# Routed experts of a two-layer model: counts loaded before the last puts, and two buffers for gathered rows

## What is computed

```python
# layer 0: 8 experts, width 1024, 4 of them for each token
router_logits = jnp.einsum('bsd,de->bse', x, router_w)
routing_weights = jax.nn.softmax(router_logits, axis=-1)
topk_weights, topk_indices = jax.lax.top_k(routing_weights, 4)
topk_weights = topk_weights / jnp.sum(topk_weights, axis=-1, keepdims=True)
h = jax.nn.gelu(jnp.einsum('bsd,edh->bseh', x, up_w))   # tanh form
expert_outputs = jnp.einsum('bseh,ehd->bsed', h, down_w)
gathered = jnp.take_along_axis(expert_outputs, topk_indices[:, :, :, None], axis=2)
output = jnp.sum(topk_weights[:, :, :, None] * gathered, axis=2)

# layer 1: 8 experts, width 1024, 2 of them for each token
gate_logits = x @ gate_w + gate_b
topk_vals, topk_idx = jax.lax.top_k(gate_logits, 2)
topk_w = jax.nn.softmax(topk_vals, axis=-1)
comb = jnp.sum(onehot * topk_w[..., None], axis=2)
h = jax.nn.gelu(jnp.einsum('btd,edf->ebtf', x, w1) + b1[:, None, None, :], approximate=False)
y = jnp.einsum('ebtf,efd->ebtd', h, w2) + b2[:, None, None, :]
output = jnp.einsum('ebtd,bte->btd', y, comb)

# the whole, for each layer
x = x + jnp.tanh(g_ffn[layer]) * ffn(_layernorm(x, axis=-1), ...)
```

## Time and profile before

| | us |
|---|---|
| median of 3 runs | 1602.8 |
| lowest and highest | 1600.75, 1604.12 |
| the profiled execution, its own time | 1604.2 |
| its span in the trace | 1602.3 |

### The profile page before, as it was taken

The page is one execution under the profiler, slowest core; times in us unless marked ns, Lnnn a source line. Parts: engine busy times, 40 slices in busy tenths (PEclk is TensorE's granted clock), DMA queues, the critical chain, the costliest instruction groups (busy, mean ns, idle before and its releaser), DMA issues. The chain is left out here.

```text
span 1602.3 us, 25436 instructions
## 1 busy us (share of the span) xinstructions
PE 1392.9 (87%) x9908; PEld 1288.8 (80%) x9908; DVE 834.8 (52%) x1654; ACT 713.1 (45%) x1375; POOL 552.5 (34%) x389
## 2 busy tenths in 40 slices
PE   5899989899867999999989995999889678987996
PEld 5776858768647899899889995988888668987996
DVE  3655656655664446446435223556666865455421
ACT  3354444444343454444444443454343425443553
POOL 1200001001025466566565441122120266566543
PEclk8899999999987999999999997998989769998998
DMA  3302031110115343443442223021202165444222
GB/s 128 120 24 67 27 95 43 52 61 27 66 51 156 94 86 81 116 106 92 105 104 47 47 42 100 24 88 41 72 30 80 54 193 119 102 106 109 48 42 35
DMA packets 72147, 123.30 MB, mean 77 GB/s; under 512 B 7440, under 2 KB 53152, under 8 KB 71968
## 3 DMA queue, kind: packets, MB, share of 16 engines
q1 hardware_dynamic: 46816, 81.92, 15.6%
q0 software_dynamic: 25152, 39.01, 13.4%
HBM read 96.12 MB, written 24.79 MB: 75 GB/s over the span
## 5 line engine op out<-in xcount | busy, mean ns | idle before, releaser
L2324 DVE TENSOR_TENSOR m_hidden_lo<-m_act_out,m_hidden_hi 128x512 fp32r<-128x512 f32 x224 | 162.6, 727 | 393.9 <-ACT m_hidden_hi L2267 368.5
L395 PE MATMUL banks<-m_down_hi,m_hidden_hi 128*128 128x256 f32 x896 | 267.9, 299 | 17.5 <-DVE m_hidden_lo L2324 11.3
L395 PE MATMUL banks<-m_down_hi,m_hidden_lo 128*128 128x256 f32 x896 | 263.7, 294 | 1.5 <-issue 1.5
L395 PE MATMUL banks<-m_down_lo,m_hidden_hi 128*128 128x256 f32 x896 | 263.9, 295 | 0.3 <-issue 0.3
L395 PEld LDWEIGHTS banks<-m_down_hi,m_hidden_hi 128*128 128x128 f32 x896 | 181.6, 203 | 22.2 <-issue 20.4
L395 PE MATMUL banks<-m_xt_hi,m_up_hi 128*128 128x256 f32 x640 | 186.6, 291 | 6.4 <-issue 6.4
L395 PE MATMUL banks<-m_xt_lo,m_up_hi 128*128 128x256 f32 x640 | 183.2, 286 | 0.0
L395 PE MATMUL banks<-m_xt_hi,m_up_lo 128*128 128x256 f32 x640 | 183.1, 286 | 0.0
L395 PEld LDWEIGHTS banks<-m_down_hi,m_hidden_lo 128*128 128x128 f32 x896 | 181.1, 202 | 1.7 <-issue 1.7
L395 PEld LDWEIGHTS banks<-m_down_lo,m_hidden_hi 128*128 128x128 f32 x896 | 181.5, 203 | 0.6 <-issue 0.6
L2401 POOL DMA_INDIRECT m_other_block<-rows,list_i x116 | 120.8, 1042 | 148.5 <-DVE list_i L1453 100.6
(11 more groups left out here) (367 smaller groups left out, 3555.0 us busy)
## 6 DMA issues: line engine op xcount, KB each, us to landing
stage<-in_down SPq DMA_DIRECT2D x22, 512.0 KB
stage<-in_ctx_cols SPq DMA_DIRECT2D x26, 402.0 KB
stage<-in_ctx_rows SPq DMA_DIRECT2D x20, 512.0 KB
stage<-in_up SPq DMA_DIRECT2D x20, 512.0 KB
m_stage<-in_up SPq DMA_DIRECT2D x11, 512.0 KB
m_stage<-in_down SPq DMA_DIRECT2D x10, 512.0 KB
rows<-xn SPq DMA_DIRECT2D x8, 528.0 KB, 3.7
stage<-in_ctx_picked SPq DMA_DIRECT2D x8, 512.0 KB
```

The costliest lines, as they stand in the source:

```text
L395: mm = q.e.matmul(dst, a, b, start=first and n == 0, stop=last and n == 2, skip_group_check=True)
L2324: q.e.tensor_tensor(lo, m.act[(n * HP + h) % ACTS], f32(hi), ALU.subtract).then_inc(*hidden_lo.mark((layer, n, h)))
```

## The change

It has two parts.

*Counts.* PE sums the counts of the last batch right after the places. VectorE casts them before mark 0 (vector_count), and each engine loads the eight registers earlier than before: PE between the count's matmul and put 0 (before: behind the 48 downs of block (0, 0)), ScalarE ahead of turning block (0, 1), VectorE when the lists are done, ahead of the next expert's casts, GpSimd before it waits for the lists. The first downs wait for put 3's sum instead of the counts' cast.

*Rows.* The blocks from 2 on take turns in two buffers: m.other for even j, and for odd j the memory of the two onehot tables, which only the route uses. Each has a semaphore and a register that counts what was begun. Block j's rows are gathered in block j - 3, so those of blocks 2 and 3 both in the opening of the expert, which is now written out in gpsimd_opening in a new order. There is one more block gathered for nearly every expert, since it is begun one block further ahead.

The diff, cut to its changed lines and a line beside them:

```diff
         stage_in = [signal(f"stage_in{i}") for i in range(6)]
-        first_in, second_in, other_in = signal("first_in"), signal("second_in"), signal("other_in")
+        first_in, second_in, other_in = signal("first_in"), signal("second_in"), [signal(f"other_in{i}") for i in range(2)]
         adding, added, other_there = signal("adding"), signal("added"), signal("other_there")
...
         lists = sb("lists", [P, E * M])
-        shared = [sb(f"onehot{i}", [P, E * P], F16) for i in range(2)]
-        onehot = [s[:, :].rearrange("p (e q) -> p e q", e=E) for s in shared]
-        pairwise = shared[0][:, :].bitcast(F32)
+        tables = sb("onehot", [P, 2 * E * P], F16)
+        shared = [tables[:, i * E * P:(i + 1) * E * P] for i in range(2)]
+        rows_there = tables[:, 0:2 * BT * ROW].bitcast(F32).rearrange("p (t d) -> p t d", t=BT)
+        onehot = [s.rearrange("p (e q) -> p e q", e=E) for s in shared]
+        pairwise = shared[0].bitcast(F32)
         above, same = (pairwise[:, i * TT * E * E:(i + 1) * TT * E * E].rearrange("p (t a b) -> p t a b", t=TT, a=E)
...
             def scales():
-                m.other = sb(n + "other_block", [P, BT, ROW], F32, st)[:, :, :]
+                m.other = [sb(n + "other_block", [P, BT, ROW], F32, st)[:, :, :], rows_there]
                 m.w_first, m.w_last = ([sb(n + f"{w}{i}", [P, BT], F32, st)[:, :] for i in range(2)] for w in ("w_first", "w_last"))
...
-        def vector_finish_lists(q, layer):
+        def vector_count(q, layer):
             use = ("count", layer)
             q.wait_ge(*route_pe.of(*use))
+            q.wait_ge(*added.of(layer - 1, "all"))
+            q.e.tensor_copy(counts_i[:, :], gen.of(use)[0:1, 0:E]).then_inc(*route_dve.mark(use))
+        def vector_finish_lists(q, layer):
             q.wait_ge(*route_dve.last())
-            q.e.tensor_copy(counts_i[:, :], gen.of(use)[0:1, 0:E]).then_inc(*route_dve.mark(use))
             spare = col("spare").unsqueeze(1).to_broadcast([P, E * NB - 1, BT])
...
             m = exp[layer]
-            return m.other if j > 1 or (e, j) == (0, 0) else m.second if j else m.first
+            return m.other[j % 2] if j > 1 or (e, j) == (0, 0) else m.second if j else m.first
...
                 return numbered(0, 0)
-            return numbered(e, j - 1) if j > 2 else numbered(e - 1, NB - 1) if j == 2 else numbered(e - 1, j)
+            return numbered(e, j - 2) if j > 3 else numbered(e - 1, NB - 4 + j) if j > 1 else numbered(e - 1, j)
...
-                q.wait_ge(*route_dve.of("count", layer))
+                q.wait_ge(*route_dve.of("put", layer, BATCH - 1, TT - 1))
             if layer and f == 0:
...
             tensor_place(q, layer, b)
+            tensor_count(q, layer)
+            held = counts(q, layer)
             for i in range(TT):
                 tensor_put(q, layer, b, i)
-            tensor_count(q, layer)
             for f in range(HT):
...
                 tensor_down(q, layer, 0, 0, f)
-            held = counts(q, layer)
             for e in range(E):
...
             scalar_choose(q, layer, b)
+            held = counts(q, layer)
             scalar_turn_block(q, layer, 0, 1)
-            held = counts(q, layer)
             for e in range(E):
...
             vector_place(q, layer, b)
+            vector_count(q, layer)
             vector_mark(q, layer, b, 0)
...
             vector_finish_lists(q, layer)
+            held = counts(q, layer)
             q.wait_ge(*rows_out[layer].of(layer, b))
...
             convert(q, "d", [quarter(layer, 1, x) for x in range(KD, 4)])
-            held = counts(q, layer)
             for e in range(E):
...
-        others_begun, adds_begun = [0], [0]
+        others_begun, adds_begun = [0, 0], [0]
         def gpsimd_gather(q, layer, e, j):
-            g, there = block_rows(layer, e, j), other_in if j > 1 else second_in if j else first_in
+            g, there = block_rows(layer, e, j), other_in[j % 2] if j > 1 else second_in if j else first_in
             q.wait_ge(*turned_block.of(layer, in_place(e, j)))
             q.wait_ge(*handed.of("w", layer, in_place(e, j)))
-            if j == 2 and (layer or e):
-                q.e.wait_ge(other_in.sem, q.e.snap(others_begun[0]))
+            if j in (2, 3) and (layer or e):
+                q.e.wait_ge(there.sem, q.e.snap(others_begun[j % 2]))
                 q.e.nop().then_inc(*rested.mark())
...
             if j > 1:
-                q.e.reg_add(others_begun[0], others_begun[0], 16 * BT)
+                q.e.reg_add(others_begun[j % 2], others_begun[j % 2], 16 * BT)
...
-            q.e.wait_ge(other_in.sem, q.e.snap(others_begun[0]))
+            q.e.wait_ge(other_in[j % 2].sem, q.e.snap(others_begun[j % 2]))
             q.e.nop().then_inc(*other_there.mark((layer, e, j)))
...
         def gpsimd_block(q, layer, e, j):
-            n, more = numbered(e, j), j == 0 and e + 1 < E
-            gpsimd_added(q, layer, n - 2)
-            if 0 < j < NB - 1:
+            n = numbered(e, j)
+            if j != 1:
+                gpsimd_added(q, layer, n - 2)
+            if j == 0:
+                gpsimd_opening(q, layer, e)
+                return
+            if 1 < j < NB - 1:
                 gpsimd_there(q, layer, e, j + 1)
-            if (e, j) == (1, 0):
+            gpsimd_add(q, layer, e, j)
+            if j + 3 < NB:
+                gpsimd_gather(q, layer, e, j + 3)
+        def gpsimd_opening(q, layer, e):
+            n, following = numbered(e, 0), [quarter(layer, e + 1, x) for x in range(4)] if e + 1 < E else []
+            gpsimd_gather(q, layer, e, 2)
+            gpsimd_gather(q, layer, e, 3)
+            if e == 1:
                 gpsimd_gather(q, layer, 2, 0)
-            if more:
-                convert(q, "p", [quarter(layer, e + 1, x) for x in range(KD)])
+            convert(q, "p", following[0:KD])
             if n:
-                gpsimd_add(q, layer, e, j)
-            if j + 2 < NB:
-                gpsimd_gather(q, layer, e, j + 2)
-            if more:
-                convert(q, "p", [quarter(layer, e + 1, x) for x in range(KD, 4)])
+                gpsimd_add(q, layer, e, 0)
+            gpsimd_there(q, layer, e, 2)
+            convert(q, "p", following[KD:4])
+            if following:
                 gpsimd_gather(q, layer, e + 1, 1)
-                if e and e + 2 < E:
-                    gpsimd_gather(q, layer, e + 2, 0)
-            if j == 0:
-                convert(q, "p", ahead(layer, e - 1))
+            gpsimd_added(q, layer, n - 1)
+            if e and e + 2 < E:
+                gpsimd_gather(q, layer, e + 2, 0)
+            convert(q, "p", ahead(layer, e - 1))
...
             own = [other_there, added]
+            held = counts(q, layer)
             q.wait_ge(*route_dve.of("listed", layer))
...
             gpsimd_gather(q, layer, 1, 0)
-            held = counts(q, layer)
             for e in range(E):
...
             gpsimd_added(q, layer, E * NB - 2)
-            q.e.wait_ge(other_in.sem, q.e.snap(others_begun[0]))
-            q.e.nop().then_inc(*rested.mark())
+            for there, begun in zip(other_in, others_begun):
+                q.e.wait_ge(there.sem, q.e.snap(begun))
+                q.e.nop().then_inc(*rested.mark())
             gpsimd_add(q, layer, E, 0)
...
         def _(e):
-            others_begun[:] = [e.alloc_register("others_begun")]
+            others_begun[:] = [e.alloc_register(f"others_begun{i}") for i in range(2)]
             adds_begun[:] = [e.alloc_register("adds_begun")]
```

## The result

| | before | after |
|---|---|---|
| median, us | 1604.08 (20 runs) | 1609.59 (20 runs) |
| lowest and highest | 1596.47, 1616.07 | 1603.27, 1618.05 |
| the profiled execution, and its span | 1604.2, 1602.3 | 1606.95, 1604.8 |

The changed kernel is slower: the ratio is 1.0037, with a 95% interval of 1.002 to 1.0054. A second comparison, in another session, gave 1.002 (1.0004 to 1.0035). So the loss is 3 to 6 us by the two ratios (0.6 to 8.7 by their intervals).

The account below looks back on a forecast made before the run. The prediction took PE, busy for 87% of the span, to bound the kernel. Its terms, -4.7 (four waits), +0.2 (layer 0's route), +3.1 (layer 1) and 0 (GpSimd's queue), gave 1602.8 - 1.4 = 1601.4 us, range 1596 to 1608.5.

Parts of the forecast that it names:

- The loads, layer 0: Layer 0's route: PE's count loads ahead of put 0 make it 4.1 us later; the route sums to +0.2 us.
- the loads' price is given back at the ups: Layer 0's route: ups only 1.2 us later, then 1.7 us regained at full clock, so -0.5 us.
- The four places: PE's waits on rows before block 3's transposes, experts 2 to 5 of layer 0: earlier gathers save 4.7 of 8.1 us.
- Rival D: The four places don't get shorter, since y and the landing of adds bound them: 1606.1 us, chance 0.09.
- Layer 1: Layer 1's route and first experts: a later PE restart and late rows together cost +3.1 us, between 0 and +5.
- the transposes of (2,0): Layer 1: GpSimd's longer queue gathers block (2,0)'s rows late, so PE waits at its transposes, +1.1 us.
- the held y: Layer 1, expert 0: ScalarE's first y waits for GpSimd, delaying PE's restart before expert 1 by +2.0 us.
- GpSimd's queue: One more pair of gathers in most experts, 2.6 us, nearly fits idle time: 0, up to +3 us.
- rival C: GpSimd's conversions collide with VectorE's hidden_lo in the openings, costing 6.6 us: slower, at 1608 us, chance 0.18.
- The sum: All terms together: -4.7 + 0.2 + 3.1 + 0 = -1.4 us for the whole kernel.

Follow-up runs that it names:

- there_first: The changed kernel with GpSimd's word that the next rows are there put ahead of its wait for the add's landing: 1605.04 us, ratio 1.0007 to the kernel before.
- after_again: The changed kernel measured once more, unaltered, against the kernel before: 1609.08 for 1604.86 us, ratio 1.002.
- rows_only: The changed kernel with its counts' half taken back, keeping two buffers, gathers three blocks ahead and the new opening: 1601.94 us, ratio 0.9988 to the kernel before.
- counts_only: The kernel before with only the counts' half of the change: 1609.59 against 1604.86 us, ratio 1.0031.
- y_early: rows_only with GpSimd's word for each layer's first y given at the start of expert 0's opening: 1600.77 us, ratio 0.998 to the kernel before.
- pe_late: The changed kernel with PE's eight loads behind the 48 downs again: 1599.01 us against 1601.78 for the kernel before, ratio 0.9971.

## Why the prediction was wrong, by its steps

**The loads, layer 0.** Put 0 was forecast 4.1 us later and came 4.2 later (8.9 behind the count's place for 4.7), the downs 3.9 later and came 4.0 later. The step that failed is the next: "the loads' price is given back at the ups: -0.5". The ups came 2.5 us later, not 1.2, because ScalarE split the turned block 2.0 us after its transposes, for 0.6 before (2.0, 1.6 and 3.0 in after, there_first and after_again, which have both halves and PE's loads early, 0.6 in all others; I have no cause that I could show). And the clock gave nothing back. The forecast took the ups at full clock; their first 4.6 us were granted 0.63 and 0.50 after, as they were before (0.63 and 0.50). PE's own time over the route, without idle time, is 37.3 and 38.9 us after, 37.5 and 39.0 before. The route cost +3.1 us, for +0.2 forecast.

**The four places.** Forecast -4.7, measured -0.9, -0.1, -0.8 and 0.0 at the waits (0.46, 2.30, 0.56 and 3.02 are left), -2.7 for the whole stretch, of which 1.4 is idle time. Two steps failed. First, I took the rows to free PE as soon as they were there, and did not ask where GpSimd says so. Its word stands behind the wait for the add, so PE stood until y started. That is shown by there_first. Second, the gain of 1.2 each rested on hidden_lo being ready 2.7 us behind y. That distance was right (710.84 to 713.60 in there_first), but the downs waited for it 2.65 and 3.81 us, because the add is as late as ever. Rival D named this, with 0.09, and the sentence "the change leaves both where they are" had it: where two things are late for one reason, removing one gives nothing. I had read SyncE's issues in the earlier trace rows, and not what released them 0.03 us before.

**Layer 1.** Forecast +3.1, measured +5.0. Of the mechanism the parts were: put 0 as in layer 0 (+3.9), the transposes of (2,0) 0.7 us late for their rows (+1.1 forecast, seen in PE's timeline as a wait of 0.73 on the gather), and the held y, which costs 2.0 us as forecast, but at another place than the step said:

```profile
1313.85 0.84 ACT L2256 ACTIVATE m_y<-banks,m_w_first 128x256 f32<-128x256 f32 x2 [5.00 <-POOLq L2436]
...
1322.19 0.69 DVE L2331 TENSOR_TENSOR m_hidden_lo<-m_act_out,m_hidden_hi 128x512 fp32r<-128x512 f32 x1 [0.70 <-ACTq L2131]
...
1323.00 0.58 PE L2162 MATMUL banks<-b,m_own 16*128 16x256 f32 x1 [1.96 <-DVEq L2131]
```

The y waits for GpSimd's word, ScalarE's chain behind it runs without a pause to the last hidden_lo, and PE's first downs of expert 1 wait for that: 1.96 us, 1.92 in after_again, no such wait before. No run tests this one by itself; it is read from the trace. The step that failed is again the loads: put 0's +3.9 came back only by 1.5 at the ups (1.60 idle for 3.08) and by 1.2 in PE's own time. And the sum had no term for the branch, which lengthened the wait before expert 1 by 1.5 us here (3.90 for 2.45). With 0.3 less at the first downs, these parts add up to +5.1.

**GpSimd's queue and rival C.** Hidden_lo instructions over 2 us rose from 4 to 6 (5 in after_again), the longest 3.4. Two more collisions of that kind can't carry the loss, and rows_only, with the new openings, shows no loss. C's time was near the truth, its mechanism was not. The row of 2.60 in the earlier trace rows shows that VectorE was held for the length of the conversion, which itself took its usual 1.94. It doesn't show that the second was held for the first: by the starts VectorE's came first.

**The sum.** Forecast +0.2 - 4.7 + 3.1 = -1.4. Measured, from the stretches with waits: +3.1 - 2.7 + 5.0 = +5.4, and the medians say +5.5 and +4.2. What the table of stretches shows beside it, some 5 us less in the rest of layer 1 after the change, doesn't stand in the medians. It is PE's own time between the transposes of (1,2) and the last ones, which lies anywhere from 206 to 214 us in the 17 profiles. It is 209.3 in counts_only, whose GpSimd has the order of before, and 214.0 in y_early, whose GpSimd has the new one. So it doesn't go with the edit. It goes with the granted clock of the stretch: 0.928 where it took 213.8, 0.956 where it took 209.3, 0.970 where it took 206.0 (pe_late). Why the clock fell differently stays open.

## What to carry to other kernels

When two engines wait for two things at nearly the same moment, look for what made both late before moving one of them: here a conversion on GpSimd handed SyncE its buffers 0.2 us ahead of GpSimd's own add, and moving that one line gave 8 to 9 us, the second buffer and three blocks' lead nothing that could be measured. A word that rows are there is worth as much as its place in the queue that gives it. Small loads to registers count on the path of an engine that is waited for, 0.66 us each on PE.

## What the runs showed of the hardware

A taken branch on PE's sequencer took 3.3 to 6.7 us, growing with what the DMA engines moved beside it (behind expert 0 of layer 1: 3.8 to 4.0 at 138 to 167 GB/s, 4.9 to 5.5 at 248 to 316, 5.5 to 6.7 at 329 to 386). The Trainium skill ("Advanced Engine Details and Errata", section "Control Flow Timing") gives about 108 ns for a compare-and-branch. Here the branches on PE that weren't taken are near that (0.07 to 0.20 us); the taken ones are 30 to 60 times as long. Each of them had a packet of 16 KB of the instruction queue inside it and ended 1.3 to 2.0 us behind that packet (272 branches), so they wait for instructions that are fetched through the DMA engines.

An indirect add of two halves at the four places landed 2.1 to 2.3 us after its end with no transfer issued beside it (five profiles that show the landing), and 4.2 to 6.8 us after it with four transfers of 400 to 512 KB issued beside its start (three profiles).
